# Slice attention: weights turned three turns behind their logits and kept turned; last pair on two PSUM banks

## The reference, cut to what matters

```python
fx_mid = (x @ W_fx + b_fx)            # per head, 64 channels
x_mid = (x @ W_x + b_x)
slice_weights = softmax((x_mid @ W_slice + b_slice) / temp, axis=-1)   # token x head x 64 slices
slice_norm = slice_weights.sum(axis=2)
slice_token = einsum('bhnc,bhng->bhgc', fx_mid, slice_weights) / (slice_norm + 1e-05)
attn = softmax((slice_token @ W_q) @ (slice_token @ W_k).T * SCALE)
out_slice = attn @ (slice_token @ W_v)
out_x = einsum('bhgc,bhng->bhnc', out_slice, slice_weights)
h = h + out_x @ W_out + b_out
```

## Time and profile before

| what | value |
|---|---|
| median of the runs | 4353.44 us |
| profiled execution, and its span | 4361.58 us, 4359.7 us |
| mean granted TensorE clock | 0.863 of full speed |
| slice attention, first logits to end of span | 3268.6 to 4359.7 us |
| TensorE busy in it | 9 tenths or more in nearly every slice, 6 in the second to fourth |

### The profile page before, as it was taken

The page is one execution under the profiler, slowest core; times in us unless marked ns, Lnnn a source line. Parts: engine busy times, 40 slices in busy tenths (PEclk is TensorE's granted clock), DMA queues, the critical chain, the costliest instruction groups (busy, mean ns, idle before and its releaser), DMA issues. The chain is left out here.

```text
span 4359.7 us, 68616 instructions
## 1 busy us (share of the span) xinstructions
PE 3178.4 (73%) x25552; PEld 1804.6 (41%) x25552; DVE 2525.0 (58%) x3049; ACT 2138.1 (49%) x3049; POOL 2575.4 (59%) x1541
## 2 busy tenths in 40 slices
PE   8999996999999940000099946676666899999997
PEld 6777774455555520000044312222221455555556
DVE  7888886888888851000055513333237777777772
ACT  6666665777777720000034335565552444444444
POOL 7777773878778716777600065555516666666661
PEclk9999998999999965555599967778777999999999
DMA  1111111122222121111133323333330111112111
GB/s 42 38 40 40 40 40 56 58 73 86 68 75 79 46 68 38 40 45 35 23 106 112 103 59 94 91 99 100 88 100 21 41 55 52 52 50 59 53 47 41
DMA packets 252194, 267.20 MB, mean 61 GB/s; under 512 B 86568, under 2 KB 168140, under 8 KB 251805
## 3 DMA queue, kind: packets, MB, share of 16 engines
q1 hardware_dynamic: 215566, 228.51, 16.8%
q0 software_dynamic: 25600, 21.10, 2.7%
q10 hardware_dynamic: 10704, 13.20, 0.9%
HBM read 127.66 MB, written 140.20 MB: 61 GB/s over the span
## 5 line engine op out<-in xcount | busy, mean ns | idle before, releaser
L1512 POOL DMA_INDIRECT D_row<-yb,D_idx x400 | 385.1, 963 | 635.8 <-DMA D_prob<-keepp 346.9
L2150 POOL TENSOR_TENSOR E_w<-E_w,E_rs 128x1024 f32<-128x1024 f32 x200 | 380.4, 1902 | 365.0 <-DVE E_rs L2073 365.0
L1241 POOL DMA_INDIRECT xb<-R_row,R_si x400 | 389.7, 974 | 212.2 <-issue 121.6
L1314 PE MATMUL X_px<-X_ident,X_xs 128*128 128x128 f32 x256 | 42.9, 291 | 559.6 <-DMA X_xs<-xb 559.6
L180 POOL TENSOR_TENSOR A_kmask<-A_ksb,A_pack_a 128x3584 f32<-128x3584 f32 x56 | 356.6, 6367 | 152.6 <-ACT A_ksb L327 152.6
L1373 ACT ACTIVATE X_hm<-X_ph,X_b 128x512 f32<-128x512 f32 x128 | 88.1, 688 | 595.6 <-PE X_ph L1326 595.6
L2058 DVE TENSOR_REDUCE E_mx<-E_lg 128x16 f32<-128x1024 f32 x200 | 244.9, 1224 | 219.6 <-PE E_lg L1867 219.3
L1388 DVE COPY X_xt<-X_px 128x512 f32<-128x512 f32 x64 | 43.6, 681 | 531.1 <-PE X_px L1314 531.1
L2144 POOL TENSOR_TENSOR E_hs<-E_w 128x512 f32<-128x512 f32 x200 | 255.1, 1275 | 93.4 <-ACT E_w L2031 93.4
L1879 PE MATMUL E_z<-E_w,E_yk 128*64 128x512 f32 (+1 forms) x800 | 224.5, 634 | 78.1 <-POOL E_w L2150 76.9
L1314 PEld LDWEIGHTS X_px<-X_ident,X_xs 128*128 128x128 f32 x256 | 27.5, 143 | 608.2 <-DMA X_b<-in_e_b 559.7
(11 more groups left out here) (292 smaller groups left out, 8394.0 us busy)
## 6 DMA issues: line engine op xcount, KB each, us to landing
xb<-B_blank SPq DMA_DIRECT2D x64, 256.0 KB, 3.9
X_xs<-xb SPq DMA_DIRECT2D x64, 256.0 KB, 2.8
yb<-X_ys SPq DMA_DIRECT2D x64, 256.0 KB, 2.0
B_x<-h SPq DMA_DIRECT2D x25, 512.0 KB, 4.2
h<-B_hh SPq DMA_DIRECT2D x25, 512.0 KB, 3.7
y<-B_yt SPq DMA_DIRECT2D x25, 512.0 KB, 2.6
R_row<-y SPq DMA_DIRECT2D x25, 512.0 KB, 3.3
A_xg<-in_xw SPq DMA_DIRECT2D x56, 224.0 KB
```

What stands on the lines that cost most here:

```text
L1241: pool.indirect_dma_start(out=xb, out_offset=bass.IndirectOffsetOnAxis(ap=si[:, B * c + b:B * c + b + 1], axis=0), in_=row[c % U][:, D * r ...
L1512: pool.indirect_dma_start(out=row[n % LR][:, k, b], out_offset=None, in_=yb, in_offset=bass.IndirectOffsetOnAxis(ap=idx[:, c, i:i + 1], ax ...
L2150: TT(w3, w3, bc(rs[g % 3][:].unsqueeze(2), [128, 2 * SH, G]), ALU.mult).then_inc(w_done, 1)
```

## The change

The weights of tile g are turned in turn g + 3, straight after its sum, and stay turned in SBUF: `wts` gets KEPT = 30 places and `w` only four. BEHIND goes from 2 to 3 and LAG to 32, so the product stays in turn g + 32. `turn_w` moves to the end of TensorE's turn; ScalarE's `wts` copies move behind the Exp of the turn. `turn_w`, product, `turn_back` and the copies take only the 65 tokens of a pair's last tile. `middle` comes one turn later. In the last pair, odd tiles use bank Z in place of O, and a product waits for the copy of the tile two before it. `shift` waits for the sum and the turning of the tile four before.

```diff
-        C, K1, BT, SLOTS, LAG, BEHIND = CHUNKS, D + 1, 4, 32, 31, 2
+        C, K1, BT, SLOTS, KEPT, LAG, BEHIND = CHUNKS, D + 1, 4, 4, 30, 32, 3
-        TURNS = TILES + LAG + 1
+        TURNS = TILES + LAG
-        wts = [m.sb(f"wts{u}", [128, 2, 512]) for u in range(2)]
+        wts = m.sb("wts", [128, KEPT, 2, 512])
+        def rows(g):
+            return TAIL if g % C == C - 1 else TILE
+        def turned_at(g):
+            return (Z if of(g)[0] == N - 1 and g % 2 else O)
+        def emptied(eng, g):
+            if of(g)[0] < N - 1:
+                after(eng, ob_done, g)
+            else:
+                after(eng, ob_done, g - 1)
         def middle(u):
-            n, m = divmod(u - C, C)
+            n, m = divmod(u - C - BEHIND + 2, C)
 # turn_w on TensorE
-                    pe.wait_ge(w_done, g + 1)
-                            last = turn(WT[:, 512 * b + 128 * k:512 * b + 128 * k + 128],
-                                        w[:, g % SLOTS, b, 128 * k:128 * k + 128], ident[:])
+                            last = turn(WT[:, 512 * b + 128 * q:512 * b + 128 * q + k],
+                                        w[0:k, g % SLOTS, b, 128 * q:128 * q + 128], ident[0:k, 0:k])
 # product
-                    after(pe, ob_done, g)
+                    emptied(pe, g)
-                            last = mm(O[HALF[b], 0:TILE], mo[n % 2][:, b, k], wts[g % 2][:, b, 128 * k:128 * k + 128],
+                            last = mm(o[HALF[b], 0:k], mo[n % 2][:, b, q], wts[:, g % KEPT, b, 128 * q:128 * q + k],
 # order on TensorE
-                    if 0 <= k < TILES:
-                        turn_w(k)
                     if u < TILES:
                         logits(u)
-                    if 0 <= k - 1 < TILES:
-                        product(k - 1)
+                    if 0 <= k < TILES:
+                        product(k)
                     if 0 <= u - BEHIND < TILES:
                         zsum(u - BEHIND)
-                    if 0 <= k - 1 < TILES:
-                        turn_back(k - 1)
+                    if 0 <= k < TILES:
+                        turn_back(k)
+                    if 0 <= u - BEHIND < TILES:
+                        turn_w(u - BEHIND)
 # ScalarE: the two wts copies leave their place ahead of tokt/mo and come behind the Exp
                         A(wf, wf, ACT.Exp).then_inc(exp_done, 1)
+                    if 0 <= k < TILES:
+                        t = rows(k)
+                        for b in range(2):
+                            act.wait_ge(wt_done[b], k + 1)
+                            after(act, o_done, k - KEPT + 1)
+                            A(wts[:, k % KEPT, b].rearrange("p (q t) -> p q t", q=SQ)[:, :, 0:t],
+                              WT[:, BANK[b]].rearrange("p (q t) -> p q t", q=SQ)[:, :, 0:t], ACT.Copy).then_inc(wtc_done[b], 1)
                     if step == 2:
 # shift on VectorE
                     if g >= SLOTS:
+                        dve.wait_ge(z_done, g - SLOTS + 1)
```

More of the change, by code:

```diff
@@ L1832, in _ @@
                 for u in range(TURNS + 1):
-                    z, left, done = u - BEHIND, u - LAG - 1, u - LAG - 2
+                    z, left, done = u - BEHIND, u - LAG, u - LAG - 1
                     if 0 <= z < TILES and closes(z):
@@ L1883, in turn_w @@
                 def turn_w(g):
-                    pe.wait_ge(w_done, g + 1)
+                    k = rows(g)
                     for b in range(2):
                         after(pe, wtc_done[b], g)
-                        for k in range(SQ):
-                            last = turn(WT[:, 512 * b + 128 * k:512 * b + 128 * k + 128],
-                                        w[:, g % SLOTS, b, 128 * k:128 * k + 128], ident[:])
+                        for q in range(SQ):
+                            last = turn(WT[:, 512 * b + 128 * q:512 * b + 128 * q + k],
+                                        w[0:k, g % SLOTS, b, 128 * q:128 * q + 128], ident[0:k, 0:k])
                         last.then_inc(wt_done[b], 1)
@@ L1893, in product @@
                     n, c = of(g)
-                    after(pe, ob_done, g)
+                    k, o = rows(g), turned_at(g)
+                    emptied(pe, g)
                     if c == 0:
@@ L1898, in product @@
                         pe.wait_ge(wtc_done[b], g + 1)
-                    for k in range(SQ):
+                    for q in range(SQ):
                         for b in range(2):
-                            last = mm(O[HALF[b], 0:TILE], mo[n % 2][:, b, k], wts[g % 2][:, b, 128 * k:128 * k + 128],
-                                      start=k == 0, stop=k == SQ - 1, skip_group_check=True)
+                            last = mm(o[HALF[b], 0:k], mo[n % 2][:, b, q], wts[:, g % KEPT, b, 128 * q:128 * q + k],
+                                      start=q == 0, stop=q == SQ - 1, skip_group_check=True)
                     last.then_inc(o_done, 1)
                 def turn_back(g):
+                    k = rows(g)
                     pe.wait_ge(oc_done, g + 1)
-                    turn(O[:, TILE:2 * TILE], oh[g % 2][:], ident[:]).then_inc(back_done, 1)
+                    turn(turned_at(g)[0:k, TILE:2 * TILE], oh[g % 2][:, 0:k], ident[:]).then_inc(back_done, 1)
                 def tokens(n):
@@ L1999, in _ @@
                 for u in range(TURNS):
-                    (n, step), k, kb = middle(u), u - LAG, u - LAG - 1
+                    (n, step), k, kb = middle(u), u - BEHIND, u - LAG
                     if step == 4:
@@ L2009, in _ @@
                         A(att[:].rearrange("p q g -> p (q g)"), M[:, BANK[0]], ACT.Copy).then_inc(attc_done, 1)
[L2010 to L2014, removed]
                     if step == 3:
@@ L2026, in _ @@
                         after(act, o_out[i % 2], 32 * (i // 2))
-                        A(ob[i % 2][:, c], O[:, TILE:2 * TILE], ACT.Copy).then_inc(ob_done, 1)
+                        A(ob[i % 2][0:rows(kb), c], turned_at(kb)[0:rows(kb), TILE:2 * TILE], ACT.Copy).then_inc(ob_done, 1)
                     if u < TILES:
@@ L2079, in leave @@
                     after(dve, back_done, g - 1)
-                    t = TILE * c
-                    STT(oh[g % 2][:], O[:, 0:TILE], bo[:], hx[i % 2][:, t:t + TILE], ALU.add, ALU.add).then_inc(oc_done, 1)
+                    t, k = TILE * c, rows(g)
+                    STT(oh[g % 2][:, 0:k], turned_at(g)[:, 0:k], bo[:], hx[i % 2][:, t:t + k], ALU.add, ALU.add).then_inc(oc_done, 1)
                 def token_norm(n):
@@ L2119, in _ @@
                 for u in range(TURNS):
-                    (n, step), k = middle(u), u - LAG - 1
+                    (n, step), k = middle(u), u - LAG
                     if step == 3:
```

## The result

The changed kernel took 4298.99 us, the median of four runs (4296.37 to 4307.09), against 4352.93 for the one before: ratio 0.987, 95% interval 0.9848 to 0.9892. The forecast was 4288 in 4276 to 4316. The mechanism of the main term was right. The gain of the middle turns was set too low and that behind the last logits too high, and the two errors cancelled in part: that the total comes near the forecast is in part luck.

A forecast was written before the change was run, and what follows sets the result against it. The prediction saw two close limits, TensorE nearly full and a ring through GpSimd. Gains of 4.8 (first turns), 35.3 (tiles 32 to 199) and 25.3 (end), total 65.4, taken from 4353.4 gave 4288 us, range 4276 to 4316.

The forecast's parts named there:

- Part 1: Sums three turns behind: the 0.50 us wait of every second turn goes, plain turns take 4.22 us, not 4.47.
- the ring: Loop from sum through logits and GpSimd's normalise to the sum of the next tile but one: 8.93 us over two turns.
- Part 2: `turn_w` moved behind `turn_back`: plain turns hold the same work; ScalarE's `wts` copies are done some 1.5 us early, hidden.
- Part 3: The six middles in tiles 32 to 199: net -1.0 us, so 40.65 each, bounds -2.5 and +2.5.
- step 2: In a middle, `zs` behind the `wts` copies: turn of 9.31 us becomes about 8.3, the next grows by about 0.9.
- step 5: A step of a middle's small attention, with a turning back; the prediction listed no change for it.
- Part 4: First 32 turns: 155.0 us becomes 150.2, gain 4.8, with the clock at 1.00 and most turns at 4.22.
- Part 5: Behind the last logits: 99.6 us becomes 74.3, gain 25.3, with the last 24 products at 1.72 each.
- rival A: The clock wavers in the first turns and the last: 11 and 6.5 us lost, time 4306; chance 0.17.
- D: Rival: the low clock stands through both ends, together 71 us lost, slower than before at 4359; chance 0.05.
- B: Rival: plain turns stay at 4.47 us, which loses 33 us, time 4321; chance 0.11.
- C: Rival: last pair's products still wait for the copy of the one before, 13 us, time 4301; chance 0.05.

The follow-up runs named there:

- e2: The kernel before with only the sums moved to three turns behind the logits (the small attention a turn later): 4300.78 us, ratio 0.9878 to the kernel before.
- e4: The changed kernel with sum and turning two turns behind the logits, not three: 4347.34 us, ratio 0.9971 to the kernel before.
- e5: The changed kernel with the last tile of a pair handled at 128 tokens in place of 65, on another chip: ratio 0.9877 to the kernel before.
- e6: The changed kernel with GpSimd's two instructions of a turn swapped, halves ahead of normalise, on another chip: ratio 0.9769 to the kernel before.
- e7: The changed kernel with 36 more transposes on TensorE in the waits of the last pair's small attention, on another chip: ratio 0.9819 to the kernel before.
- e10: e7 again, now beside the changed kernel on one chip: 4283.33 us, ratio 0.9817 to the kernel before.
- e3: The changed kernel with all products and turned results in one bank, O: 4321.3 us, ratio 0.9927 to the kernel before.

## Why the prediction was right, and where it was not

**Part 1, right, mis-sized.** The waits for `normalise` were the ring; e2 and e4 show it from both sides (41.7 and 47 us). The plain turn was taken as 4.22 and came out as 4.18 on average: TensorE's own turn is 4.07, and GpSimd's 4.21 the bound. 131 turns make 5 us of it. The 4.21 of the earlier trace rows was taken as a floor for every turn; turns of 4.07 stand beside it.

**Part 2, right for the copies it names.** No wait of TensorE for ScalarE's `wts` copies or the slots of `w` appeared. But one wait for ScalarE did, which the prediction had named as a sign of being wrong: behind the middles the copy to `ob` waits for its store (six times between 3428 and 4211 us, up to 4.7 us), and three products wait for the copy, 2.6 us in all. e2 has three such waits too.

**Part 3, right within its bounds, by errors that cancel.** Middles of 39.1 to 40.3 us were forecast as 40.65. In the middle of the sixth pair step 2 fell from 9.31 to 8.17 us, as forecast. The turn behind it grew by 1.8, not 0.9, and step 5, forecast unchanged, fell from 9.95 to 9.02. The multiply of the scores did not pay for its later start. The timeline of the changed kernel, against the earlier trace rows:

```profile
4010.07 2.35 DVE L2135 TENSOR_TENSOR E_at<-E_at,E_ars 128x256 f32<-128x256 f32 x2
4010.70 1.43 POOL L2163 TENSOR_TENSOR E_hs<-E_w 128x512 f32<-128x512 f32 x1
```

It ended 0.29 us behind `halves` again (4012.42 against 4012.13), as the rule of the Trainium skill on the shared ports has it (SBUF — State Buffer, Who interferes with whom). It is 0.5 shorter because it started nearer to that end. The cut of the last tile, counted as 0.5 a middle, is worth nothing (e5).

**Part 4, right.** 149.5 against 150.2, the clock at 1.00, the ring of 4.21 in the first turns. e6 took that ring out and the first 32 turns fell to 138.7.

**Part 5, the step that failed.** The last 24 products were to take 41.4 and took 44.3 to 49.0. Of this, 24 x 0.09 = 2.2 is the step from turning back to product, 0.25 to 0.26 in place of 0.17: the 0.17 was read between two transposes, and what makes a product start later was not tried. The timeline of the changed kernel, against the earlier trace rows:

```profile
4299.51 1.09 PE L1916 MATMUL E_o<-E_wts,E_mo 128*64 128x128 f32 x16
4301.06 0.33 PE L1923 MATMUL E_o<-E_pack_f,E_oh 128*128 128x128 f32 x1 [0.46 <-DVE E_oh L2100]
4301.31 0.69 PE L1916 MATMUL E_z<-E_wts,E_mo 128*64 128x65 f32 x16
```

The rest is the clock, and with it the attention ahead: 35.7 to 39.3, not 32.9. The prediction priced the turning there as work removed and the clock at 1.00. The turning also filled waits: in the kernel before the clock stood at 1.00 in that stretch, in e2, with the turning in its old place, at 0.96 (35.8 us), in the changed kernel it fell further or for longer, and with fillers e7 and e10 had 1.00 again, and 32.9 us, just the forecast, then 43.7. The missing turning is thus a part of the cause, not all of it. At the full clock the sums of this part hold but for the 2.2. This is rival A in part; and what the prediction held against rivals A and D, that a busier TensorE gets the clock back, does not hold in the last turns: e5 stood at 1.2 GHz for all of them with a share of 0.84.

**The sum.** Forecast 65.4 us; by stage spans 62.4, 71.0 and 68.0 in three profiles. Middle turns gave 10 more than forecast, 5 in the plain turns and 4 in the middles; the end gave 6 to 14 less. The prediction's own range was too narrow for its bounds: six middles at +3.5 each are 21 us, which reaches 4309, not 4298. Rivals B and C did not happen; C's one bank, run as e3, cost 32, not 13, again for the clock.

Open: why the same last products run at 1.81 or at 2.83. Busy shares don't sort it: 0.75 went with 1.00 (e10) and with 0.50 (e3), 0.84 with 0.50 (e5). Whether whole tiles made e5 slow, or chance, is not shown; the two groups of its own runs speak for chance.

## What to carry to other kernels

When a wait goes, look for every ring that closes within a few hundredths of the new turn: here 4.07 of TensorE and 4.21 of GpSimd with VectorE, and opening the second one (an exchange of two lines) took another 34 us off, half of what the whole change gave. Work that is moved out of an engine's idle stretches may have been what held its clock; price such a stretch at both clock levels, not only as work saved. And a turn that shows no idle time is not yet a floor: this one lost 0.14 us more once the sum stood a turn later.

## What the runs showed of the hardware

The same sequence of products and turned results stood for 68 us at 1.2 GHz with TensorE busy 0.84, and for 44 us at 2.4 GHz busy 0.75: both persist, and a low clock makes a stretch look busier, since each instruction takes longer (a product 1.98 against 1.09 us). With one bank the clock fell from 1.00 within 20 us and stayed at 0.50 to the end, at 3.27 to 3.31 us a turn. VectorE's multiply of two SBUF operands took 2.35 to 2.85 us beside GpSimd's instructions and 0.76 without them.
